# Whole scans of 1024 steps, four decay banks, two turning banks, and a two-step softplus in a Mamba and mixture-of-experts kernel

## The reference

```
x     = silu(causal_conv(xz))                        # 512 channels
delta = softplus(dbc[..., :64] @ Wdt.T + b_dt)
Bm, Cm = dbc[..., 64:80], dbc[..., 80:96]            # 16 states
dA = exp(delta[..., None] * A)
bx = delta[..., None] * Bm[:, :, None, :] * x[..., None]
def step(h, inp):
    dAi, bxi, ci = inp
    h = dAi * h + bxi
    return (h, jnp.einsum('ben,bn->be', h, ci))
```

## Time and profile before

| | |
|---|---|
| median of 3 runs | 4276.8 us (4267.73 to 4282.5) |
| profiled execution, time | 4277.29 us |
| profiled execution, span | 4276.1 us |
| PE busy | 3526.6 us, 82% |
| DVE busy | 3719.1 us, 87% |
| ACT busy | 3137.2 us, 73% |
| POOL busy | 3641.0 us, 85% |
| mean granted TensorE clock | 0.911 of full |

### The profile page before, as it was taken

The page is one execution under the profiler, slowest core; times in us unless marked ns, Lnnn a source line. Parts: engine busy times, 40 slices in busy tenths (PEclk is TensorE's granted clock), DMA queues, the critical chain, the costliest instruction groups (busy, mean ns, idle before and its releaser), DMA issues.

```text
span 4276.1 us, 58098 instructions
## 1 busy us (share of the span) xinstructions
PE 3526.6 (82%) x18160; PEld 2545.2 (60%) x18160; DVE 3719.1 (87%) x4584; ACT 3137.2 (73%) x5280; POOL 3641.0 (85%) x2205
## 2 busy tenths in 40 slices
PE   6677687989779898798978988898987889878986
PEld 2444465666556655467555774656755576557866
DVE  5999998998998989989899898979989898898931
ACT  6667576887758877689776887668876787768843
POOL 5999988999878989789988899889988889889831
PEclk8888797999979998899988999899998999989998
DMA  4433332656335654257543674436753466426656
GB/s 136 126 110 103 119 123 97 201 192 220 123 101 176 220 179 151 99 184 230 182 146 111 195 253 147 146 119 220 230 168 110 142 212 213 156 102 196 199 205 213
DMA packets 374654, 700.87 MB, mean 164 GB/s; under 512 B 31809, under 2 KB 205386, under 8 KB 370378
## 3 DMA queue, kind: packets, MB, share of 16 engines
q1 hardware_dynamic: 362058, 663.59, 46.9%
q0 software_dynamic: 12288, 33.57, 2.4%
HBM read 527.72 MB, written 169.35 MB: 163 GB/s over the span
## 4 chain that ended last, share of the span: by engine, by line
DVE 28%; PE 27%; issue 15%; POOL 14%; ACT 12%; DMA 4%; DVEq 0%; SPq 0%; another core or an unknown queue 0%; POOLq 0%; ACTq 0%
DVE h L1489 10%; DVE h L1486 7%; POOL drive L2016 7%; PE h_t L1259 5%; PE side L1293 5%; DVE y L1498 5%; ACT decay L1731 3%; POOL y L2034 3%; PE side L1434 2%; PE side L1426 2%; POOL drive L2022 1%; PE side L1277 1%; DVE stats L1553 1%; PE side L1300 1%; PE side L1397 1%
## 5 line engine op out<-in xcount | busy, mean ns | idle before, releaser
L2016 POOL TENSOR_TENSOR drive<-xu,b_row 128x1024 f32<-128x1024 f32 x960 | 2260.0, 2363 | 181.8 <-DVE h L1489 87.2
L1731 ACT ACTIVATE decay<-delta,neg_a 128x512 f32<-128x512 f32 x2048 | 1383.1, 691 | 468.9 <-DVE h L1489 286.1
L1259 PE MATMUL h_t<-ident,h 128*128 128x128 f32 x8192 | 1243.4, 298 | 455.3 <-DVE h L1489 178.4
L1259 PEld LDWEIGHTS h_t<-ident,h 128*128 128x128 f32 x8192 | 1039.3, 153 | 803.0 <-DVE y L1498 223.7
L1498 DVE SCALAR_TENSOR_TENSOR y<-h_t,c_col,y 128x512 f32<-128x512 f32 x1368 | 996.9, 729 | 119.1 <-PE h_t L1259 107.5
L2034 POOL TENSOR_TENSOR y<-y,scaled 128x512 f32<-128x512 f32 x616 | 785.3, 1275 | 80.8 <-ACT scaled L1752 80.3
L1489 DVE TENSOR_TENSOR_SCAN h<-decay,h,drive 128x512 f32<-128x512 f32 x512 | 652.8, 1275 | 15.7 <-ACT decay L1731 3.7
L1489 DVE TENSOR_TENSOR_SCAN h<-decay,drive 128x512 f32<-128x512 f32 x512 | 618.5, 1208 | 39.2 <-ACT decay L1731 24.2
L1486 DVE TENSOR_TENSOR_SCAN h<-decay,h,drive 128x512 f32<-128x512 f32 x448 | 571.8, 1276 | 39.6 <-ACT decay L1731 29.2
L1486 DVE TENSOR_TENSOR_SCAN h<-decay,drive 128x512 f32<-128x512 f32 x448 | 541.7, 1209 | 52.6 <-ACT decay L1731 32.5
L1752 ACT ACTIVATE scaled<-h_t,c_col 128x512 f32<-128x512 f32 x616 | 415.7, 675 | 65.5 <-PE h_t L1259 64.9
(11 more groups left out here) (304 smaller groups left out, 4337.7 us busy)
## 6 DMA issues: line engine op xcount, KB each, us to landing
expert_w<-in_w SPq DMA_DIRECT2D x344, 512.0 KB, 4.6
b_row<-b_dram SPq DMA_DIRECT2D x240, 512.0 KB
x_dram<-xu SPq DMA_DIRECT2D x16, 2048.0 KB, 10.1
delta_dram<-prep_work SPq DMA_DIRECT2D x60, 512.0 KB, 3.1
delta<-delta_dram SPq DMA_DIRECT2D x60, 512.0 KB, 5.3
ys_dram<-work SPq DMA_DIRECT2D x40, 512.0 KB, 6.6
work<-xs_dram SPq DMA_DIRECT2D x38, 512.0 KB, 5.2
prep_work<-xz_dram SPq DMA_DIRECT2D x32, 512.0 KB
```

The lines of the kernel that those rows point to most:

```text
L1259: t = pe.e.transpose(h_t[i % N_H_T][:, c * P:(c + 1) * P], its_h[:, c, :], ident[:, :])
L1731: act.e.activation(decay[:, i % N_DECAY, :], delta[:, c, its], ACT.Exp, scale=neg_a[:, c, w % 2, n:n + 1]).then_inc(decay_made, 1)
L2016: op = pool.e.tensor_tensor(drive[:, k % N_DRIVE, :], xu[:, w % 2, c, :], b_row[:, row % N_B_ROW, :], ALU.mult)
```

## The change

- A unit of the first 15 walks is scanned by one instruction of 1024 steps. It reads two neighbouring decay banks as one row of 1024; the four banks make two such pairs. It waits for both decays of its unit, and starts from zero, so that the two halves no longer hand a state over. `scan_rest` and `first_scanned` are gone. The units of the last walk are still scanned by halves (`scan_half`).
- `N_DECAY` goes from 3 to 4 and `N_H_T` from 3 to 2. A decay waits for the whole unit that used its bank before it, two units back. ACT's decays go out three slots ahead of their slot instead of two (`N_DECAY - 1`).
- Softplus is two ACT operations, exp(v) and ln(1 + .), and the DVE operation takes max(v, min(that, 17)).
- `AT`, `BANK_USE`, `FIRST_EW`, `B1_AT` and `ZERO_AT` have new numbers for all side work. `TAIL_USE` is the same.
- Two waits are added: `xn_copy` waits for the `xn_store` of the batch before, and `x1_load` for the `x1_load` of the batch before.

```diff
-N_DECAY = 3
+N_DECAY = 4
-N_H_T = 3
+N_H_T = 2
...
             def scan_unit(k):
-                dve.wait_ge(decay_made, NH * k + 1)
+                dve.wait_ge(decay_made, NH * k + NH)
                 dve.wait_ge(drive_made, k + 1)
...
+                at = NH * k % N_DECAY
+                its_decay = decay[:, at:at + NH, :].rearrange("p r t -> p (r t)")
+                back = slice(None, None, -1 if (gn // N) % 2 else 1)
+                dve.e.tensor_tensor_scan(h[:, gn % 2, c, back], its_decay[:, back], drive[:, k % N_DRIVE, back],
+                                         0.0, ALU.mult, ALU.add).then_inc(scanned, 1)
...
-            def scan_rest(k):
-                dve.wait_ge(decay_made, NH * k + NH)
-                if k < WHOLE:
-                    dve.wait_ge(first_scanned, k + 1)
-                scan(k, 1).then_inc(scanned, 1)
...
-                    if odd:
-                        scan_rest(k)
-                    else:
+                    if k >= WHOLE:
+                        scan_half(k, odd)
+                    elif not odd:
                         scan_unit(k)
...
+                place = i % N_DECAY
+                if k < WHOLE:
+                    place = (NH * k + its.start // BANK) % N_DECAY
                 if i >= N_DECAY:
-                    before, its_r = divmod(i - N_DECAY, NH)
-                    act.wait_ge(scanned if its_r else first_scanned, before + 1)
-                act.e.activation(decay[:, i % N_DECAY, :], delta[:, c, its], ACT.Exp,
+                    act.wait_ge(scanned, (i - N_DECAY) // NH + 1)
+                act.e.activation(decay[:, place, :], delta[:, c, its], ACT.Exp,
...
-                    act.e.activation(log_part, side[bank_of["dt_mm", index]][:, :], ACT.Abs).then_inc(soft_step, 1)
-                    act.wait_ge(soft_step, done_before + 1)
-                    act.e.activation(log_part, log_part, ACT.Exp, scale=-1.0).then_inc(soft_step, 1)
-                    act.wait_ge(soft_step, done_before + 2)
+                    act.e.activation(log_part, side[bank_of["dt_mm", index]][:, :], ACT.Exp).then_inc(soft_step, 1)
+                    act.wait_ge(soft_step, nth("softplus", w, c, s))
                     op = act.e.activation(log_part, log_part, ACT.Ln, bias=1.0)
```

The tables change throughout. The end of the list for `xn_copy`, in 256ths of a slot, shows the size of the moves (422144 is slot 1649, 419072 is slot 1637):

```diff
-        354816, 354817, 417280, 417536, 422144, 422145],
+        351233, 353792, 353793, 416768, 416769, 419072, 419073],
```

More of the change, by code:

```diff
@@ L478 @@
[L478 to L480 removed]
+    "tok_var": [-254, -251, 25346, 27650, 87552, 97793, 151042, 160256, 217088, 222208, 284672, 288772, 349952,
+        353280, 415744, 418304, 526082, 526092, 526095, 526101],
+    "neg_a": [-35817],
+    "tok_rstd": [-35840, -35839, 25088, 27648, 89344, 98304, 151040, 160512, 217088, 222208, 284672, 288768,
+        350208, 353280, 415232, 418304, 525825, 525829, 525830, 525831],
@@ new lines @@
+    "cw_make": [-35838, -35836, -35835, -35834, 2048, 4608, 6144, 7680],
+    "xn_copy": [-35836, -35835, -35834, -35833, 26624, 28928, 29184, 29440, 92928, 94208, 101376, 101377,
+        154112, 156673, 161280, 161792, 218880, 219136, 225536, 225537, 285440, 288512, 289792, 289793, 351232,
+        351233, 353792, 353793, 416768, 416769, 419072, 419073],
+    "d_make": [-35837],
+    "cw_store": [-35825, -35820, -35818, -35813, -35810, -35807, -35803, -35794],
+    "proj": [1540, 1541, 1542, 1543, 1544, 1545, 1546, 1547, 29696, 30208, 32256, 32257, 34304, 34816, 36352,
[4 rows of a table added]
@@ new lines @@
+    "dt_mm": [1553, 1554, 1555, 1556, 1557, 1558, 1559, 1560, 13058, 14592, 19456, 19457, 20992, 20993, 23040,
[9 rows of a table added]
+    "softplus": [-35810, -35809, -768, -767, -766, -765, -764, -763, 15616, 15872, 20224, 20225, 20992, 21504,
[9 rows of a table added]
+    "delta": [-242, -241, -240, -239, -238, -237, -236, -235, 16384, 16385, 20480, 20481, 22016, 22017, 23808,
[9 rows of a table added]
+    "x_store": [-35819, -35797, -35755, -35703, -35637, -35559, -35493, -35409, -35347, -35250, -35186, -35092,
+        -35023, -34943, -34879, -34787],
+    "b_store": [-35817, -35796, -35745, -35694, -35629, -35533, -35474, -35395, -35324, -35251, -35148, -35066,
+        -34990, -34940, -34848, -34757],
@@ new lines @@
+    "rank_mm": [90624, 161026, 230657, 294145, 361728, 427008, 491520, 525853],
+    "mix_turn": [90112, 90368, 161792, 161793, 230144, 230145, 295424, 295937, 361984, 364032, 426752, 426753,
+        492800, 494338, 525863, 525864],
+    "eo_mm": [90625, 90880, 91648, 91649, 93696, 94208, 94209, 94210, 162304, 162305, 166656, 166912, 170752,
[4 rows of a table added]
+    "slots": [90624, 161280, 230912, 294400, 361984, 427008, 491776, 526105],
+    "mix_copy": [89857, 90624, 162048, 162049, 230400, 230912, 295425, 296960, 362240, 363523, 426753, 426754,
+        492800, 495617, 525604, 525608],
@@ L558 @@
+    "tok_apply": [1155, 1156, 1166, 1168],
 }
+SOFT_MAX = 17.0
 TAIL_USE = 1153
@@ new lines, in scan_unit @@
+                gn, c = divmod(k, EC)
+                if gn >= 2:
+                    dve.wait_ge(turned, (gn - 1) * TB)
+                at = NH * k % N_DECAY
[3 more added lines that the diff above has]
+                                         0.0, ALU.mult, ALU.add).then_inc(scanned, 1)
@@ new lines, in scan_half @@
+            def scan_half(k, r):
+                hs, part, n, _ = half_state(k)
+                c = k % (EC // NH) * NH + r
+                dve.wait_ge(decay_made, NH * k + r + 1)
+                dve.wait_ge(drive_made, k + 1)
+                if hs < 4:
+                    dve.wait_ge(turned, (SPLIT * N - 1 + hs // 2) * TB)
+                else:
+                    dve.wait_ge(turned, SPLIT * TILES + (hs - 3) * QB)
+                    dve.wait_ge(h_kept, min(hs - 3, N))
+                if part:
+                    dve.wait_ge(h_kept, n + 1)
+                op = dve.e.tensor_tensor_scan(h_half(hs)[:, c, ::-1], decay[:, (NH * k + r) % N_DECAY, ::-1],
+                                              drive[:, k % N_DRIVE, r * BANK:(r + 1) * BANK][:, ::-1],
+                                              carried_h[:, n, c:c + 1] if part else 0.0, ALU.mult, ALU.add)
+                if r == NH - 1:
+                    op.then_inc(scanned, 1)
@@ L1535, in side_piece @@
                     into = prep_half if w else delta[:, c, :]
-                    op = dve.e.scalar_tensor_tensor(out=into[:, half_of], in0=side[bank_of["dt_mm", index]][:, :],
-                                                    scalar=0.0, in1=log_parts[:, half_of], op0=ALU.max, op1=ALU.add)
+                    op = dve.e.scalar_tensor_tensor(out=into[:, half_of], in0=log_parts[:, half_of], scalar=SOFT_MAX,
+                                                    in1=side[bank_of["dt_mm", index]][:, :], op0=ALU.min, op1=ALU.max)
                 elif piece in ("tok_stats", "ln_stats"):
@@ L1757, in side_piece @@
                     act.wait_ge(done["xn_turn"], nth("xn_turn", b, s, c))
+                    if b:
+                        act.wait_ge(done["xn_store"], 16 * nth("xn_store", b - 1))
                     if b >= 2:
@@ L2348, in transfer @@
                     sp.wait_ge(x1_out[0], 16 * (b + 1))
+                    if b:
+                        sp.wait_ge(done["x1_load"], 16 * nth("x1_load", b - 1))
                     if b == LAST:
```

309 lines of the change are left out of this document (125 added, 184 removed), and 692 rows, old and new, of tables (AT, BANK_USE).

## The result

| | before | after |
|---|---|---|
| median (lowest to highest) | 4277.7 us (4267.7 to 4282.5) | 4220.4 us (4217.1 to 4227.7) |
| span of the profiled execution | 4276.1 us | 4217.4 us |
| scans, first to last | 65.35 to 4060.64 us | 67.63 to 4000.00 us |

The ratio is 0.9871 [0.9849, 0.9894]: 57 us faster, with 112 forecast. The direction and the range held the result, the size did not. All of it lies where the scans run, 3995.3 us before and 3932.4 after, 63 us less; what lies ahead of them and behind them takes 4 us more.

The account below looks back on a forecast made before the run. DVE was taken as the main bound with POOL close behind. Scans 125 plus softplus 12 minus turned tiles 25 made 112 us less, 4165 us (2.6% less); own range 4125 to 4205 us, 8 in 10 4085 to 4262.

Parts of the forecast that it names:

- What bounds the kernel: Scan phase, 3995.3 us: DVE the main bound, busy 3644 us, with POOL close behind at 3557 us.
- Scans of 1024: DVE, 960 units: one scan instead of two halves saves 120 us plus 46 us of state hand-over, 166 us of DVE's time.
- What of the saving reaches the end: Scan phase: three quarters of DVE's 166 us, 125 us, become time; POOL's drive is late next, then the decays.
- Decay banks: ACT's decays: average lead about the same, costed at nothing; ends 50 us less wait and 80 us more.
- Turning banks: PE's turned tiles: lead lost with two banks, 25 us more waits; ends -20 and +172.
- Softplus: ACT: one operation gone 128 times, 12 us less in all; ends 3 and 35.
- Turned tiles as the bound: Rival, DVE's sum behind PE's side work: 86 waits grow by 2 us each, 172 us, giving 4312 us; chance 0.10.
- Coarser hand-over: Rival, banks given back once in 2.2 us: 75 decay waits grow, 80 us, giving 4245 us; chance 0.20.
- The whole gain: Rival: POOL's waits take up the difference, 202 + 12 = 214 us saved, giving 4063 us; chance 0.15.
- What would show it: Signs in the trace after: 2.27 us scans, DVE busy about 3580 us, h_t waits 110 to 150 us; over 200 wrong.

Follow-up runs that it names:

- a_light: Kernel after with half of PE's side work in convolution and the experts' two products left out: 0.9747 of before.
- b_light: Kernel before with the two-step softplus and half of PE's side work in convolution and the experts' two products left out: 0.9859 of before.
- w_o2: Kernel after with both decays of a unit in one bank, the scan reading one element of it 1024 times, two turning banks: 4233.2 us, 0.9875.
- w_o3: The same as w_o2 but with three turning banks, places unchanged: 4228.0 us, 0.9862.
- Experiment 6: Kernel of w_o3, but PE turns both tiles of a unit before the slot's side work: 4223.1 us with three turning banks, 4223.0 with four.
- a_both: Kernel after without half of PE's side work in convolution and the experts' products and without seven eighths of POOL's adds: 0.9596 of before.
- b_both: Kernel before with two-step softplus, the same cuts to PE's side work and POOL's adds as a_both: 0.9789 of before.
- w_t4: Kernel of w_o3 with four turning banks, PE turning both tiles of a unit before the slot's side work: 4223.0 us, 0.9863.

## Why the forecast was right in direction and wrong in size

**What bounds the kernel.** "DVE as the main bound with POOL close behind" was an average over the scan phase and over two first walks. By stretch of a batch DVE leads clearly in one of four and by a point in another. The prediction read windows, but not these; the trace of the kernel before alone would have shown PE at 93% beside DVE at 84% in three sixteenths of the tiles. That would have warned of the loss there, though not priced it: with PE brought down to 83% (a_light beside b_light) the stretch still paid 1 us of 18.

**Scans of 1024:** right. 166 us forecast and 157 measured, the duration 2283 ns against 2270, no cost of reading two banks as one row. By the forecast's own terms, start to start, the merged instruction gave 960 x (1.132 + 1.195 - 2.202) = 120 us, as forecast, and the hand-over of the state 37 instead of 46: 199 second halves came right behind the first, not 240, at 1.318 us instead of 1.132 (the 21 us of the account above are the idle part of that alone). What wasn't priced is 21 us more for sums and side work on DVE; the sum's mean is 736 ns against 729. A part of it is the new order: a sum behind another sum takes 746 ns and one behind a scan 732, and before the change all but 5 of the 1368 sums stood behind a scan. In w_o2 and w_o3 the mean is 732 and 731, so another part differs from one chip or run to the next, and the rest I can't name.

**What of the saving reaches the end:** this step failed. "Three quarters, 125 us" rested on POOL's 145 us of waits as slack. Of the DVE busy time saved in the six batches, 89 us, 44 came out as time: half. The prediction had POOL's drives late next, then the decays. But DVE's waits for drives grew by 6 us only and those for decays fell; what grew were those for turned tiles and for PE's side products, by 76 and 33 us. Without softplus the forecast had 100 us (125 - 25) and the runs show 38; easing POOL alone brings this to 66, easing PE alone to 48, easing both to 83, so the neighbours together hold it, and even then only about half of 157 us is had.

**Decay banks:** forecast at nothing; the waits fell by 29 us, and halves with a fourth bank are 32 us faster. Within the bounds (50 us less), with the wrong value. By coming out better than forecast it hid a part of what the step before had too high: luck.

**Turning banks:** 25 us more waits forecast, 72 measured (107.5 to 179.5). The step's size and its mechanism were wrong: lead by banks is worth 5 us in the kernel after and 16 under halves, and the waits hardly change with it (175.4 and 176.0 us; 229.2 and 211.4). That whole scans bring the two sums of a unit next to each other stands in the prediction, but as a gain for PE at a state's first tile; that the odd tile loses its cover does not. And the sum treated a wait as a price. Experiment 6 took 65 us of it away, and no gain can be told.

**Softplus:** 12 forecast, 17.5 measured, give or take 7: right.

**The rivals.** Turned tiles as the bound (4312 us) did not come, though the waits went 72 us of the 172. Coarser hand-over named 4245 us; the result lies nearer to it than to the forecast, but its mechanism, longer waits for decays, isn't there: they fell. The whole gain fell with the traces. The rule of the Trainium skill (Perfetto Trace Analysis, "Optimizing Scalar/DVE Operations"), that smaller instructions may let work end sooner where Vector isn't saturated but causes bubbles on others, would have whole scans cost time in the first and third stretches (DVE at 84% in both). In the third the time was the same within 0.6 us in six batches, in the first it was 20 us shorter, so the trace shows no loss by the larger instruction in either.

**What would show it,** point by point: scans as told; DVE busy 3606.6 us (forecast 3580); POOL's waits for scans 71 us (50); waits for h_t 179.5 us (110 to 150, with over 200 called wrong); ACT 94 us less (80).

**What stays open.** With both neighbours eased DVE still waits 52 us more for tiles in a_both than in b_both, and some 70 us of the saving aren't had. Whether that is the longer round of four engines around a unit of 2.2 us, or the lists of places, these runs don't tell: no list of places was tried that fits both lengths. The old places with four decay and two turning banks weren't tried under whole scans.

## What to carry to other kernels

Before you convert an engine's saved time into time of the kernel, cut the run at equal work into its recurring stretches and compare the engines there. That shows where a saving may be lost, but the shares don't give its fraction: here the stretch where DVE led by 10 points paid 72%, one where it didn't lead paid all, and another nothing. A wait isn't a price: where several engines are near 90%, removing one (here 65 us) can just move it to the next semaphore. And when two instructions become one, look for whose lead the gap between them had covered (here the odd tile's), and expect a hand-fitted schedule to hold for its own instruction length alone (166 us worse under halves, 62 us better under whole scans).

## What the runs showed of the hardware that I had not expected

A scan's duration was linear within 0.5% from 64 steps over 512 to 1024: 2283 ns measured, 2273 by 2.080 ns a step from the two shorter ones. Decays in two banks as one row cost no more than that line gives, and one element read 1024 times takes 2279 ns (w_o2). And work taken from PE seems to be partly given back by its clock: with half of the side work left out the mean granted clock is 0.882 and 0.884 of full instead of 0.906 and 0.915, and a transposition takes 306 to 308 ns on average instead of 298 or 299, 8192 times. The clock's part in this isn't isolated: the order of the turns moves the mean too, to 294 ns in w_t4 at a clock of 0.910.
